# A gated recurrence stage: ACT's gated function for logistic and product, products in pairs by kind, sums of squares in 32-row strips, roots by group

## The reference, cut to what matters

```
i = x @ Wi.T ; f = x @ Wf.T ; g = x @ Wg.T      # x: layer norm, [8, 256, 256]
gate = sigmoid(f)
i_in = silu(i) * (1 - gate)
o_t  = gate_t * o_(t-1) + i_in_t                 # scan along the 256 tokens of a sequence
rms  = rsqrt(mean(g*g, over the width) + EPS)
x    = x + (g * rms * g_norm_weight * (o * sigmoid(o))) @ Wo.T
```

## Time and profile before

| | |
|---|---|
| median of 3 runs | 845.12 us (844.83 to 847.11) |
| the profiled execution | 842.05 us, its span on the core 840.1 us |
| PE busy | 738.6 us, 88% |
| DVE busy | 481.7 us, 57% |
| ACT busy | 403.6 us, 48% |
| the stage: first product to last addition | 183.89 to 259.16 us of the span |

### The profile page before, as it was taken

The page is one execution under the profiler, slowest core; times in us unless marked ns, Lnnn a source line. Parts: engine busy times, 40 slices in busy tenths (PEclk is TensorE's granted clock), DMA queues, the critical chain, the costliest instruction groups (busy, mean ns, idle before and its releaser), DMA issues.

```text
span 840.1 us, 13928 instructions
## 1 busy us (share of the span) xinstructions
PE 738.6 (88%) x3946; PEld 497.3 (59%) x3946; DVE 481.7 (57%) x1816; ACT 403.6 (48%) x963; POOL 281.0 (33%) x296
## 2 busy tenths in 40 slices
PE   5999999989898999999966899997899888799970
PEld 3446777554465456777543378666667665378640
DVE  5663333478866663333379653335997866753336
ACT  3822433317643722333246436543788777436530
POOL 0572333400000572433306725550011133635550
PEclk9999999999999999999985999999999999899995
DMA  8843333199999943333195245526000011245528
GB/s 301 270 169 119 106 108 104 58 300 351 351 350 350 352 145 119 105 110 105 58 368 219 107 124 166 156 94 200 1 1 1 2 54 41 94 126 171 155 95 300
DMA packets 99295, 134.62 MB, mean 160 GB/s; under 512 B 11494, under 2 KB 88294, under 8 KB 98662
## 3 DMA queue, kind: packets, MB, share of 16 engines
q1 hardware_dynamic: 85782, 95.97, 36.5%
q0 software_dynamic: 13440, 37.77, 12.2%
HBM read 54.85 MB, written 78.84 MB: 159 GB/s over the span
## 4 chain that ended last, share of the span: by engine, by line
PE 66%; DVE 16%; ACT 7%; DMA 4%; issue 4%; POOL 1%; SPq 0%; POOLq 0%; DVEq 0%; ACTq 0%
PE bank L1030 19%; PE bank L1051 11%; PE bank L926 11%; PE bank L1003 4%; PE bank L939 3%; PE bank L1040 3%; PE bank L1113 3%; DVE X L1348 2%; DVE st L1366 2%; DVE X L1352 2%; PE bank L1164 2%; PE bank L866 2%; DMA Y<-f_result_rows 2%; PE bank L1232 1%; PE bank L1140 1%
## 5 line engine op out<-in xcount | busy, mean ns | idle before, releaser
L517 POOL DMA_INDIRECT f_result_rows<-arena x152 | 146.2, 962 | 209.2 <-ACT arena L676 195.5
L517 POOL DMA_INDIRECT slot_rows<-XN,slots x128 | 123.9, 968 | 239.2 <-DVE slots L1480 177.8
L1030 PE MATMUL bank<-w,arena 128*128 (+3 forms) x800 | 176.9, 417 | 2.2 <-ACT arena L661 0.7
L1668 DVE COPY arena<-bank 88x128 f32<-88x128 f32 (+1 forms) x224 | 56.1, 284 | 155.8 <-PE bank L1040 148.7
L1030 PEld LDWEIGHTS bank<-w,arena 128*128 128x128 f32 (+1 forms) x800 | 103.9, 164 | 41.5 <-issue 15.7
L926 PE MATMUL bank<-XT,f_s 128*128 128x512 f32 (+1 forms) x256 | 122.9, 628 | 1.6 <-ACT arena L676 1.0
L1051 PE MATMUL bank<-w,arena 88*128 (+3 forms) x576 | 118.3, 380 | 1.6 <-DVE arena L1668 1.6
L669 ACT ACTIVATE arena<-bank 128x128 f32<-128x128 f32 (+1 forms) x152 | 45.1, 296 | 106.7 <-PE bank L1030 105.7
L676 ACT ACTIVATE arena<-bank 128x256 f32<-128x256 f32 x152 | 58.5, 385 | 59.6 <-PE bank L1051 59.3
L926 PEld LDWEIGHTS bank<-XT,f_s 128*128 128x128 f32 (+1 forms) x256 | 48.3, 197 | 58.5 <-issue 55.7
L1051 PEld LDWEIGHTS bank<-w,arena 88*128 88x128 f32 (+3 forms) x576 | 71.1, 167 | 14.8 <-issue 4.3
(11 more groups left out here) (178 smaller groups left out, 1078.5 us busy)
## 6 DMA issues: line engine op xcount, KB each, us to landing
slot_rows<-zeros SPq DMA_DIRECT2D x16, 2312.0 KB, 20.1
arena<-slot_rows SPq DMA_DIRECT2D x104, 136.0 KB
XN<-f_result_rows SPq DMA_DIRECT2D x32, 256.0 KB, 5.5
Y<-f_result_rows SPq DMA_DIRECT2D x32, 256.0 KB, 6.0
arena<-slot_rows SPq DMA_DIRECT2D x96, 68.0 KB
w<-in_f_w SPq DMA_DIRECT2D x1, 4096.0 KB, 15.7
w<-in_f_w SPq DMA_DIRECT2D x1, 2816.0 KB
f_result_rows<-arena POOLq DMA_INDIRECT x152, 2.4
```

What stands on the lines that cost most here:

```text
L517: pool.indirect_dma_start(out=dst, out_offset=bass.IndirectOffsetOnAxis(ap=idx, axis=0), in_=src, in_offset=None).then_inc(done.sem, 16)
L1030: last = pe.matmul(bank[2 + q % 2][lanes, 0:2 * m.H], xsT[q % 2][:, k, lanes], L["w13"][:, k, e, :], start=(k == 0), stop=(k == KD - 1))
L1668: last = dve.tensor_copy(hT[q % 2][0:kp, k, :], bank[4 + q % 2][0:kp, k * P:(k + 1) * P])
```

## The change

ACT's Silu takes the place of a sigmoid and a DVE product, once for i and once for o; the DVE products L1705 and L1719 go. Silu lies in a third table. PE makes the products of a group in pairs, f f i i g g, and ACT reads them in that order. The first two products no longer wait for the additions of the stage before; those of i do, and so the last group of those additions reads banks 4 and 5 in place of 2 and 4 (down_bank). squares has the ones stationary (128x32) and the squared tile moving, each tile of tokens into its own 32 rows of bank 1; ACT copies these rows out, PE transposes them back (squares_back), and ACT takes the root of a group from there. The root comes for each group: that of group g-1 at the end of ACT's turn g, behind stdev. DVE scales the tiles of group g+2 after back(g), and project_out of group 2 now comes before the squares of group 3.

```diff
@@ -389,7 +390,11 @@
         def down_bank(s, g, half):
             held = g - HELD[s["kind"]]
-            return bank[(6, 7)[half] if held < 0 or held % 2 == 0 else (2, 4)[half]]
+            return bank[(6, 7)[half] if held < 0 or held % 2 == 0 else (4, 5)[half]]
+
+        def gate_bank(g, k, c):
+
+            return bank[2 + (3 * KD * g + KD * k + c) % 4]
         def known(j):
             return isinstance(j, int)
@@ -703,56 +708,75 @@
                     shared_silu(n)
             def recurrence(s):
-                def first(g):
+                def forget(g):
                     for c in range(KD):
                         n = KD * g + c
-                        f, i, gate = (bank[2 + (3 * n + k) % 4][:, :] for k in range(3))
                         act.wait_ge(*s["f_psum"](n + 1))
                         if g:
                             act.wait_ge(*s["scan"](n - KD + 1))
-                        act.activation(g_keep[c], f, ACT.Sigmoid).then_inc(s["keep"].sem, 1)
-                        act.activation(g_in[c], f, ACT.Sigmoid, scale=-1.0).then_inc(s["in_"].sem, 1)
-                        if c and g + 1 < NG:
-                            copy_pair(s, g + 1, 0, 0)
...
-                        act.activation(g_si[c], i, ACT.Sigmoid).then_inc(s["si"].sem, 1)
...
+                        act.activation(g_keep[c], gate_bank(g, 0, c)[:, :], ACT.Sigmoid).then_inc(s["keep"].sem, 1)
+                        act.activation(g_in[c], gate_bank(g, 0, c)[:, :], ACT.Sigmoid, scale=-1.0).then_inc(s["in_"].sem, 1)
+
+                def squares(g):
+
+                    act.wait_ge(*s["ms_psum"](g + 1))
+                    if g:
+                        act.wait_ge(*s["ms_back"](g))
+                    act.activation(g_rows, bank[1][:, 0:P], ACT.Copy).then_inc(s["ms_rows"].sem, 1)
+
+                def inputs(g):
+                    for c in range(KD):
+                        act.wait_ge(*s["i_psum"](KD * g + c + 1))
+                        act.activation(g_si[c], gate_bank(g, 1, c)[:, :], ACT.Silu).then_inc(s["si"].sem, 1)
+
+                def gate(g, c):
+                    n = KD * g + c
+                    act.wait_ge(*s["g_psum"](n + 1))
+                    if g >= 2:
+                        act.wait_ge(*s["ms_psum"](g - 1))
+                    act.activation(g_sq[:, g % 2, c, :], gate_bank(g, 2, c)[:, :], ACT.Square).then_inc(s["sq"].sem, 1)
+                    if g:
+                        act.wait_ge(*s["t"](n - KD + 1))
+                    act.activation(g_gw[c], gate_bank(g, 2, c)[:, :], ACT.Copy, scale=hnorm[:, c:c + 1]).then_inc(s["gw"].sem, 1)
+
+                def output(g):
                     for c in range(KD):
                         n = KD * g + c
                         act.wait_ge(*s["scan"](n + 1))
                         if g:
                             act.wait_ge(*s["t"](n - KD + 1))
-                        act.activation(g_so[c], g_o[c], ACT.Sigmoid).then_inc(s["so"].sem, 1)
+                        act.activation(g_so[c], g_o[c], ACT.Silu).then_inc(s["so"].sem, 1)
+
+                def mean_squares(g):
+
+                    act.wait_ge(*s["ms_back"](g + 1))
+                    act.activation(g_ms[:, GT * g:GT * (g + 1)], bank[1][:, P:2 * P].rearrange("p (t q) -> p t q", q=Q)[:, :, 0],
+                                   ACT.Sqrt, scale=1.0 / D, bias=epsc[:, :]).then_inc(s["ms"].sem, 1)
                 act.activation(unused[:, :], epsc[:, :], ACT.Sqrt)
                 loaded(act, "h")
                 stdev(s, 0)
                 copy_pairs(s, 0, (0, 1))
-                stdev(s, 1)
                 for g in range(NG):
-                    first(g)
+                    forget(g)
+                    if g == 0:
+                        stdev(s, 1)
+                    else:
+                        squares(g - 1)
+                    inputs(g)
+                    if g + 1 < NG:
+                        copy_pair(s, g + 1, 0, 0)
+                    gate(g, 0)
+                    if g + 1 < NG:
+                        copy_pair(s, g + 1, 1, 0)
+                    gate(g, 1)
+                    output(g)
                     if g + 2 < NG:
                         stdev(s, g + 2)
-                    if g == 2:
-                        mean_squares(0)
-                    second(g)
-                mean_squares(1)
+                    if g:
+                        mean_squares(g - 1)
+                squares(NG - 1)
+                mean_squares(NG - 1)
...
@@ -1100,35 +1124,58 @@
             def recurrence(s):
                 loaded(pe, "h")
+                released = [s["in_"], s["in_"], s["si"], s["si"], s["gw"], s["gw"]]
+
+                def product(g, k, c):
+                    w, psum = (("wf", s["f_psum"]), ("wi", s["i_psum"]), ("wg", s["g_psum"]))[k]
+                    m = 3 * KD * g + KD * k + c
+                    if m >= 4:
+                        before_g, order = divmod(m - 4, 3 * KD)
+                        pe.wait_ge(*released[order](KD * before_g + order % KD + 1))
+                    for kk in range(KD):
+                        last = pe.matmul(gate_bank(g, k, c)[:, :], hw[w][:, kk, c * P:(c + 1) * P],
+                                         XT[:, kk, g * GW:(g + 1) * GW], start=(kk == 0), stop=(kk == KD - 1))
+                    last.then_inc(psum.sem, 1)
+
+                def next_pair(g, h):
+                    pe.wait_ge(*s["xT"](2 * g + h))
+                    transpose_pair(s, g, h, 0)
+
                 def project(g):
                     pe.wait_ge(*s["xT"](2 * (g + 1)))
+                    product(g, 0, 0)
+                    product(g, 0, 1)
+                    if g:
+                        squares(g - 1)
+                    else:
+                        pe.wait_ge(*s["prev"]["shared_added"](NTT))
+                    product(g, 1, 0)
+                    product(g, 1, 1)
+                    if g:
+                        squares_back(g - 1)
+                    if g + 1 < NG:
+                        next_pair(g + 1, 0)
+                    product(g, 2, 0)
+                    if g + 1 < NG:
+                        next_pair(g + 1, 1)
+                    product(g, 2, 1)
+
+                def squares(g):
+
+                    pe.wait_ge(*s["sq"](KD * (g + 1)))
+                    if g:
+                        pe.wait_ge(*s["ms"](g))
                     for c in range(KD):
...
-                def squares(g):
-
-                    if g == 2:
-                        pe.wait_ge(*s["ms"](1))
-                    pe.wait_ge(*s["sq"](KD * (g + 1)))
-                    for t in range(GT):
-                        for c in range(KD):
-                            last = pe.matmul(bank[1][:, GT * g + t:GT * g + t + 1], g_sq[:, g % 2, c, t * P:(t + 1) * P], ones[:, 0:1],
+                        for t in range(GT):
+                            last = pe.matmul(bank[1][t * Q:(t + 1) * Q, 0:P], ones[:, 0:Q], g_sq[:, g % 2, c, t * P:(t + 1) * P],
                                              start=(c == 0), stop=(c == KD - 1))
                     last.then_inc(s["ms_psum"].sem, 1)
+
+                def squares_back(g):
+
+                    pe.wait_ge(*s["ms_rows"](g + 1))
+                    pe.transpose(bank[1][:, P:2 * P], g_rows, ident[:, :]).then_inc(s["ms_back"].sem, 1)
@@ -1143,13 +1190,13 @@
                 transpose_pair(s, 0, 0, 0)
                 transpose_pair(s, 0, 1, 1)
-                pe.wait_ge(*s["prev"]["shared_added"](NTT))
                 for g in range(NG):
                     project(g)
                     if g >= 2:
                         project_out(g - 2)
+                project_out(NG - 2)
                 squares(NG - 1)
-                project_out(NG - 2)
+                squares_back(NG - 1)
                 project_out(NG - 1)
                 keep_busy(24, 0)
@@ -1702,10 +1749,8 @@
                     for c in range(KD):
                         n = KD * g + c
                         dve.wait_ge(*s["si"](n + 1))
-                        dve.tensor_tensor(g_t1[c], g_si[c], bank[2 + (3 * n + 1) % 4][:, :], ALU.mult).then_inc(s["t1"].sem, 1)
+                        dve.tensor_tensor(g_t1[c], g_si[c], g_in[c], ALU.mult).then_inc(s["t1"].sem, 1)
                         dve.wait_ge(*s["t1"](n + 1))
-                        dve.tensor_tensor(g_t1[c], g_t1[c], g_in[c], ALU.mult).then_inc(s["t2"].sem, 1)
-                        dve.wait_ge(*s["t2"](n + 1))
                         for b in range(GW // S):
                             seq = slice(b * S, (b + 1) * S)
                             last = dve.tensor_tensor_scan(g_o[c][:, seq], g_keep[c][:, seq], g_t1[c][:, seq], 0.0,
@@ -1716,19 +1761,17 @@
                     for c in range(KD):
                         n = KD * g + c
                         dve.wait_ge(*s["so"](n + 1))
-                        dve.tensor_tensor(g_so[c], g_o[c], g_so[c], ALU.mult).then_inc(s["t3"].sem, 1)
```

(44 more changed lines are left out.)

17 lines of the change are left out of this document (removed).

## The result

The changed kernel takes 837.84 us (median of 11 runs, 835.47 to 842.62), the kernel before in the same comparison 845.12 us (11 runs, 841.75 to 847.11). The ratio is 0.9916, with a 95% interval of 0.9897 to 0.9935: faster by 0.8%. The profiled execution took 838.12 us, its span was 836.3 us. Some executions of a kernel fall into a slower state (3 of the 13 of before in the comparison with e1 to e4); medians here are of all executions, ratios of the others alone.

A forecast was written before the change was run, and what follows sets the result against it. The prediction took the recurrence stage to be bound by a loop between ACT and DVE for groups 0 and 1 and by PE for groups 2 and 3. Its stretch terms summed to -7.75, 845.12 to 837.4 us, range 834.3 to 841.5.

The forecast's parts named there:

- From root of group 1 to combine of group 2: Stretch from ACT's root to DVE's combine: 9.43 us becomes 6.08, with f products and sigmoids over before the root; -3.35.
- I count nothing, for ACT then waits at the root of group 1: Stage start: PE's f products begin some 1.5 us earlier, not waiting for shared_add; counted as no gain.
- lost cover: Stage start: if ACT's wait at the root of group 1 no longer hid PE's early start, 1.5 us more.
- From root of group 2 to combine of group 3: Path goes through ACT's root, loads, sigmoids, row copy and Silu, then DVE's front: 10.19 us becomes 9.59; -0.60.
- From root of group 3 to the first output tile: PE's squares of group 1 wait for ACT's root of group 0: 9.01 us becomes 9.16; +0.15.
- a lower clock after PE's waits: Rival: PE's clock falls behind its new wait before the squares of group 1; +1.5 us, total 838.9, chance 0.18.
- PEclk at 0.50 between 215 and 235: Sign that the prediction is wrong: PE's clock at half speed between 215 and 235 us.
- From the first output tile on: Three stretches, to group 3's first product, group 1's outputs and the last addition: -2.12, -1.07 and -0.76.
- the rival in which they run one after another: Rival: the strips of squares on PE cost 1.84 us as the old form; +3.8, total 841.2, chance 0.05.
- the estimate of +9.7: By the skill's rule, seven table loads on ACT's new path cost 1.38 us more each: kernel at 847.
- ACT becomes the bound: Rival: table switches cost more on a path through seven loads; +9.0 us with loads doubled, total 846.4, chance 0.05.
- Zeroing: Rival: POOL's first scatter, due at 264.7 us, is held by the zeroing; gain lost, total 845, chance 0.02.

The follow-up runs named there:

- e1: Changed kernel with 20 transposes of the identity put on PE ahead of the squares of group 1, filling its wait; stage 70.47 us, whole 877.17 us.
- e4: Changed kernel with only the strips undone, squares by one-column matmuls, no row copies or transposes back; stage 76.10 us, whole 885.09 us.
- after_again: The changed kernel run again with no edit; stage 70.47 us, whole 836.9 us in one run.
- e5: Changed kernel with PE's first two products again waiting for the additions of the stage before; stage 75.13 us, whole 841.14 us against 844.39.
- e6: Kernel before with Silu for both sigmoids and 16 DVE products out, old order kept; stage 90.75 us, whole 855.9 us, ratio 1.014.
- e7: Changed kernel with group 0's sums in bank 6 and ACT's next layer-norm root moved before Silu; stage 66.84 us, whole 833.41 us, ratio 0.9869.
- after_third: The changed kernel run a third time with no edit; stage 72.16 us, whole 885.96 us in one run.
- before_again: The kernel before, profiled again with no edit; stage 79.75 us, whole 887.24 us.
- e8: Changed kernel with the roots of groups 0 and 1 taken together in ACT's turn of group 2; stage 72.39 us, whole 887.11 us.
- e3: Changed kernel with Silu undone, sigmoids and DVE's 16 products back, new order kept; stage 73.37 us, whole 876.05 us against 880.64, ratio 0.9959.
- e2: Changed kernel with group 0's transposed sums in bank 6, so group 1's squares need not wait for ACT's root; stage 70.51 us, whole 875.32 us.

## Why the prediction was right

**The total.** Forecast 837.4, measured 837.84. The medians differ by 7.28, the sum said 7.75. The profiled pair differs by less, 842.05 to 838.12, that is 3.9: the stage took 5.97 less, and the rest of the execution 2.0 more. The remainder, the execution less its stage, was 764.0 before and 766.0 after. In four profiles on a chip where the kernel before takes as long (844.39) it was 766.4 (after_again), 766.0 (e5), 765.5 (e6) and 766.3 (e7), so the first profile of before probably had a short one by some 2 us. Taking the sum from the median was right. But the gap of 3.1 between median and profile was no property of the kernel: for the changed kernel it is 0.3 and the other way, so the profiled execution, forecast at 834.3, took 838.12. That the median came within 0.44 is in part luck, since a fall of the clock that the sum left out costs some executions of the changed kernel 1.6 us and some of the kernel before 1.7.

**From root of group 1 to combine of group 2** (-3.35, measured 6.05 for 6.08). It holds for the reason given, sigmoids over before the root, but by 0.27 us only. e5 shows that 3.0 of it hang on PE's early start. The clause "I count nothing, for ACT then waits at the root of group 1" was right in its sum and did not say that the term above it rested on the same start; the price it named for lost cover, 1.5, was half, since the clock at the entry is the other half.

**From root of group 2 to combine of group 3** (-0.60, measured 9.60 for 9.59). ACT's chain of root, load, sigmoids, copy, load, Silu. e7 confirms that it is ACT: with the root out of the head of that chain the stage gets 3.6 shorter.

**From root of group 3 to the first output tile** (+0.15, measured 10.77 for 9.16). The step that failed is the one that left the clock at full speed behind PE's new wait. The rival "a lower clock after PE's waits" took place in this execution and in after_third, not in after_again: 1.6 us (10.77 - 9.16), priced at 1.5 with a chance of 0.18. Its mechanism and price were right. Its chance was too low: with e4 and e5 it took place in four of five executions with that wait. The reading that the clock did not fall behind the wait of 1.88 rested on a single execution: in before_again it did, for 1.7 us. PEclk at 0.50 between 215 and 235 was also one of the signs by which the prediction called itself wrong, and it came. How much of the fall is left in the ratio, now that either kernel can have it, no run tells.

**From the first output tile on** (-2.12, -1.07, -0.76; measured 3.50, 11.19 and 13.37 for 3.48, 11.02 and 13.37). e8 puts the root back and finds 5.57, so the first of these is shown. The 0.87 for an output tile isn't what 5.49 / 6 gives (0.92), but four tiles took 3.50, 0.875 each. The strips are 16 records in 0.64 at full clock, as taken; e4 finds 2.2 us for the form over the stage, less than the 3.8 of the rival in which they run one after another, because transposes and row copies go with them.

**Loads.** Fourteen, one of them ahead of the stage, at 1283 ns each. The root's end and the load's start, and the load's end and the Silu's start, lie 0.02 and 0.01 us apart in the rows of after. The Trainium skill, "ScalarE: Activation LUTs", section "What ACT_TABLE_LOAD costs", adds some 1380 ns of drain to each switch; no row here shows it, and the measurement decides. The Trainium skill, "ScalarE: Activation LUTs", section "Table sets: the hidden batching unit", asks for calls to be batched by set, and e6 bears it out, +12.7 us where the function adds fifteen loads to the old order; e7, with as many loads as after, is no case of it.

The working counted its loads wrongly. It speaks of seven on the new path, in the estimate of +9.7 and in the rival "ACT becomes the bound", and of five added ones that are "in the sum". The sum itself holds three, two behind roots and one ahead of Silu, and the last alone is new. The rows of after bear the three out (188.96, 199.99 and 203.54); the others fit into ACT's waits. So both prices count four loads too many.

**Zeroing and serial strips** didn't occur: POOL's first scatter came at 266.36, 13.28 us behind the end of the stage, where before it was 13.27 (272.43), and the strips kept their 0.64.

**What stays open**: what decides in a given execution whether the clock falls behind a wait; why it cost more in e4; and whether a later stage gives a little back. Behind the stage it took 580.9 us before and 583.2 after, 614.4 in before_again and 618.1 in after_third. Against it stand the medians, which differ by 7.28, and after_again, which is 7.5 under its median of before with a stage 7.6 shorter.

## What to carry to other kernels

When an activation with its own table takes over an elementwise product, count the table loads of the new order first: the function is worth having only where the calls of one kind stand together, and the root of a norm belongs where its input is ready when ACT comes to it (e7: as many loads, 3.6 us less). Lay the path out by stretches between named starts; a wait of the engine that looks busiest may cost nothing while the engine that ends it holds the loop, and filling or moving the wait (two small edits) tells which. An early start that seems hidden can be what makes the next term true, so take it away by itself before calling it free.

## What the runs showed of the hardware

The granted clock of PE behind the same wait of 2.57 or 2.58 us fell in two executions of the changed kernel, in e4 and in e5, and stayed at full speed in after_again; behind 1.88 us it stayed up in before and e6 and fell in before_again. It fell behind the 2.14 to 2.21 us at the entry in before, before_again, e5 and e6, and behind 3.09 us in e3. The pair of i products took 5.15 and 5.40 where it fell (6.19 in e4) and 3.70 where it didn't. In e1, where PE was kept busy, in e7, where the wait was gone, and in e2 and e8, with waits of 1.84 and 1.85 at other places, no fall showed behind them. In the rows of after an ACT table load begins 0.01 to 0.03 us behind the end of the activation ahead of it and takes 1.28 us, and the next activation, where its input is there, starts 0.01 us behind the load; the 23 loads in e6's stage have the same mean, 1283 ns. Sixteen 128x128 matmuls with 32 columns of ones stationary took 0.64 us, sixteen one-column ones with the data stationary 1.84.
